# Two GNN layers on one core: the operands of the degree count change places

## The chip, the cores and the metric

The kernel runs on one NeuronCore of a Trainium2 chip. The metric is the device time of one execution in microseconds; three runs of the kernel before gave 4552.12 us in the median (4550.2 to 4552.79). The profile is another execution, taken with the hardware profiler on.

## The reference

The network has two layers on 6250 nodes with 256 features and 106,250 edges (each of 50,000 drawn pairs in both directions, and a loop for each node, sorted by destination). A layer is a graph part plus a linear-attention part, each on the layer-normalised features, and then a feed-forward part with experts. The change touches the graph convolution of the first layer alone:

```
out_deg = segment_sum(ones, src)          # edges that leave each node
in_deg  = segment_sum(ones, dst)
norm_src, norm_dst = rsqrt(max(out_deg, 1)), rsqrt(max(in_deg, 1))
x   = features * norm_src @ W_gcn         # 6250 x 64
agg = segment_sum(x[src], dst)
h   = relu(agg * norm_dst + b_gcn) @ W_out + b_out
```

To gather rows of `x`, the kernel must first have `out_deg`: for each node, how often it occurs in the list `src`.

## The kernel before, in words

Nodes lie in 49 tiles of 128 (W = 49, P = 128): node number = 128 * high part + low part. The edge list has 832 columns of 128 edges (GB = 832), padded with a node number that no tile holds. The kernel is a row of stages with a barrier of all engines between two of them. The first is the class `Front`; behind it come `Prelude` (keys and values of the attention, first groups of edges), `fold0`, `Stage1`, a table stage, `Stage2`, the router's table and `Stage3`. Each engine has its own list of instructions, written out by hand, and semaphores order them against each other.

Front does four things beside each other: it normalises the 49 node tiles, transposes them and multiplies them by W_gcn; it counts `src` into degrees; it sorts out which 128-edge blocks belong to which node tile; and it writes the table from which edges gather.

The degree count (lines 697 to 703 and 823 to 832) goes in 52 rounds, called halves in the code, of 16 columns of edges (BAT = 16). In each, VectorE (DVE) writes two one-hot tiles in bf16: `ohlo` [128, 128, 16] compares each edge's low part with 0..127 (L827), `ohhi` [128, 49, 16] its high part with 0..48 (L830). The 16 columns are the innermost axis of both, so that one column's one-hot is read at a step of 16 elements. Both tiles are doubled: round h may be written when round h - 2 has been used (`s_used`). TensorE (PE) then takes `degree(h)`: 16 products, one per column, that add up in one PSUM bank `deg`. In a product the first operand is loaded into the array as weights, the second streams through it. `deg` is opened by a product of zeros (L719) that sets all its entries.

PE's list in Front is: the zero product, then for h = 0 to 51 `degree(h)`, and from h = 3 (TILE_AT) on, behind it, `tile(h - 3)`: two f32 transposes of the next node tile (L223, into `pt`) and the two f32 products by W_gcn (L714, four matmul instructions in the trace). At three rounds there are small products for the sorting into the bank `pz` (L729 to L738). ScalarE (ACT) copies transposes and products out of PSUM (L211, L763), normalises the next tile (L772) and, in the first half of the stage, counts edges per tile by the sign function (L757, 49 times). SyncE (SP) stores each transposed tile to memory.

DVE's list, from h = 2 on: at given rounds other work (layer-norm statistics of the next seven tiles, the bias rows, the sorting), then the two one-hots of round h. When the last round is used it takes the maximum of `deg` with 1 (L1000), ScalarE the root (L798), DVE the reciprocal into `nsrc` (L1005, [128, 49]: low part on the partitions, high part along the row). Between maximum and reciprocal DVE does `put(0)` and `put(1)` (L939, L940): casts of the slot lists that PE transposes at the end of its list (L744, L745). After the reciprocal the 49 x 64 products are scaled by `nsrc` and stored as the table in seven blocks.

Of the kernel before, what the change touches and what calls it, by code (L numbers as in the profile page):

```python
# [10 lines left out]
ALU = mybir.AluOpType  # L11
ACT = mybir.ActivationFunctionType
# [3 lines left out]
P = 128  # L16
# [3 lines left out]
W = -(-N // P)  # L20
# [125 lines left out]
class Norm:  # L146
# [71 lines left out]
    def tensor(self, t, i, j):  # L218
        t.wait_ge(self.s_xn, TPI * i + j + 1)

        t.wait_ge(self.s_xr, TPI * i + (j - 1 if j >= 2 else 0))
        for c in range(C):
            mm = t.transpose(self.pt[:, j % 2, c * P:(c + 1) * P], self.xn[:, j, c * P:(c + 1) * P], self.R.ident[:, :])  # L223
        mm.then_inc(self.s_tp, 1)
# [321 lines left out]
class Front:  # L546
# [10 lines left out]
    def __init__(self, f, nc, R, A):  # L557
# [24 lines left out]
        self.ohhi = f.sb("ohhi", [P, 2, W, self.BAT], BF16)  # L582
        self.zero = f.sb("zero", [P, P], BF16)
        self.std = f.sb("dstd", [P, W])
        self.wext = f.sb("wext", [P, C, GCN])
        self.gsum = f.sb("gsum", [P, C, 2 * HEADS])
        self.bsum = f.sb("bsum", [PARTS, 2 * HEADS])
# [107 lines left out]
    def tensor(self, t):  # L695
        R, nm = self.R, self.nm

        def degree(h):
            t.wait_ge(self.s_hot, 2 * h + 2)
            for b in range(self.BAT):  # L700
                mm = t.matmul(self.deg[:, 0:W], self.ohlo[:, h % 2, :, b], self.ohhi[:, h % 2, :, b], start=False,
                              stop=False, skip_group_check=True)
            mm.then_inc(self.s_used, 1)

        def tile(n):
            i, j = divmod(n, TPI)
            if n + 1 < W:
                t.wait_ge(nm.s_xt, n + 1 if j + 1 == TPI else n)
                nm.tensor(t, *divmod(n + 1, TPI))
            t.wait_ge(nm.s_xt, n + 1)  # L710
            if n >= 2:
                t.wait_ge(self.s_ec, n - 1)
            for c in range(C):
                mm = t.matmul(self.pext[:, n % 2, 0:GCN], nm.xt[:, nm.place(i, j), c], self.wext[:, c, :], start=(c == 0),  # L714
                              stop=(c == C - 1))
            mm.then_inc(self.s_ep, 1)

        t.wait_ge(self.s_zeroed, 1)
        t.matmul(self.deg[:, 0:W], self.zero[:, :], self.zero[:, 0:W], start=True, stop=False, skip_group_check=True)  # L719
        for h in range(self.HALVES):  # L720
            degree(h)
            if h == self.TILE_AT:
                t.wait_ge(self.s_w, 16)
                nm.tensor(t, 0, 0)
            if h >= self.TILE_AT:
                tile(h - self.TILE_AT)
            if h == self.COUNT_AT:
                t.wait_ge(self.s_counted, 1)
                t.matmul(self.pz[:, 0:W], R.ones[:, :], self.cnt[:, :], start=True, stop=True).then_inc(self.s_summed, 1)  # L729
            if h == self.KEYS_AT:  # L730
                t.wait_ge(self.s_keyed, 1)
                for k in range(3):
                    t.transpose(self.pz[0:W, k * P:(k + 1) * P], self.row[:, k, :], R.ident[:, :])
                t.transpose(self.pz[0:W, 3 * P:4 * P], self.key[:, :], R.ident[:, :]).then_inc(self.s_columns, 1)
            if h == self.RANKS_AT:
                t.wait_ge(self.s_moved, 1)
                for k in range(3):
                    mm = t.matmul(self.pz[:, k * W:(k + 1) * W], self.col[0:W, k, :], self.move[0:W, :], start=True, stop=True)  # L738
                mm.then_inc(self.s_ordered, 1)
        for j in range(self.J):  # L740
            t.wait_ge(self.s_split, 2 * (j + 1))
            if j >= 2:
                t.wait_ge(self.s_put, 2 * (j - 1))
            t.transpose(self.pt[:, j % 2, 0:P], self.srcf[:, j], R.ident[:, :])  # L744
            t.transpose(self.pt[:, j % 2, P:2 * P], self.dstf[:, j], R.ident[:, :]).then_inc(self.s_turned, 1)  # L745
# [3 lines left out]
    def scalar(self, a):  # L749
        R, nm = self.R, self.nm  # L750
        self.w = 0

        def signs(n):
            for w in range(self.w, min(self.w + n, W)):
                if w:
                    a.wait_ge(self.s_signed, w)
                a.activation(self.junk[:, :], self.dstw[:, :], ACT.Sign, bias=self.edge[:, w:w + 1],  # L757
                             accum_out=self.cnt[:, w:w + 1]).then_inc(self.s_signed, 1)
            self.w = min(self.w + n, W)

        def taken(n):
            a.wait_ge(self.s_ep, n + 1)
            a.activation(self.xw[:, n, :], self.pext[:, n % 2, 0:GCN], ACT.Copy).then_inc(self.s_ec, 1)  # L763

        def normalise(i, j):
            if i >= ITER:
                return
            n = TPI * i + j
            a.wait_ge(nm.s_rstd, i + 1)
            if i:  # L770
                a.wait_ge(nm.s_tp, n - TPI + 1)
            a.activation(nm.xn[:, j], R.X[:, n, :], ACT.Identity, bias=R.less[:, n:n + 1],  # L772
                         scale=nm.rstd[:, j:j + 1]).then_inc(nm.s_xn, 1)

        a.wait_ge(self.s_cut, 1)
        signs(8)
        nm.scalar_root(a, 0)
        for j in range(TPI):
            normalise(0, j)
        for n in range(W):  # L780
            i, j = divmod(n, TPI)
            if i >= self.SETS:
                a.wait_ge(self.s_ep, TPI * (i - self.SETS) + j + 1)
                a.wait_ge(self.s_xd[nm.place(i, j)], 16 * (i // self.SETS))
            nm.scalar_copy(a, i, j)
            if n:
                taken(n - 1)
            signs(2)
            if j == 1 and i + 1 < ITER:
                nm.scalar_root(a, i + 1)  # L790
            if j >= 2:
                normalise(i + 1, j - 2)
            if j == TPI - 1:
                normalise(i + 1, j - 1)
                normalise(i + 1, j)
        taken(W - 1)
        a.wait_ge(self.s_maxed, 1)
        a.activation(self.std[:, :], self.std[:, :], ACT.Sqrt).then_inc(self.s_rooted, 1)  # L798

        def cast(i, k):  # L800
            if 0 <= i < ITER:
                x = self.xw[:, TPI * i:TPI * (i + 1), :]
                if k == 0:
                    a.wait_ge(self.s_scaled, i + 1)
                    if i >= self.TABS:
                        a.wait_ge(self.s_out[i % self.TABS], 16 * (i // self.TABS))
                else:
                    a.wait_ge(self.s_less, i + 1)
                a.activation(self.tabt[:, i % self.TABS, :, k * GCOL:k * GCOL + GCN], x, ACT.Copy)\
                    .then_inc(self.s_cast[k], 1)  # L810

        for i in range(ITER + 1):
            cast(i, 0)
            cast(i - 1, 1)
# [3 lines left out]
    def vector(self, v):  # L818
        R, nm, J, last = self.R, self.nm, self.J, W - 1
        st = Steps(v, self.s_st)  # L820
# [114 lines left out]
        def put(j):  # L935
            if j >= J:
                return
            v.wait_ge(self.s_turned, j + 1)
            v.tensor_copy(R.gsrc[:, j * P:(j + 1) * P], self.pt[:, j % 2, 0:P]).then_inc(self.s_put, 1)  # L939
            v.tensor_copy(R.gdst[:, j * P:(j + 1) * P], self.pt[:, j % 2, P:2 * P]).then_inc(self.s_put, 1)  # L940
# [56 lines left out]
                split()  # L997
            one_hots(h)
        v.wait_ge(self.s_used, self.HALVES)
        st.then(v.tensor_scalar(self.std[:, :], self.deg[:, 0:W], 1.0, None, ALU.max))  # L1000
        v.sem_inc(self.s_maxed, 1)
        put(0)
        put(1)
        v.wait_ge(self.s_rooted, 1)
# [2640 lines left out]
```

## Time and profile before

| | |
|---|---|
| median of 3 runs | 4552.12 us |
| span of the profiled execution (its only time) | 5387.9 us |
| PE busy | 3828.0 us, 71% |
| DVE busy | 3145.7 us, 58% |
| POOL busy | 2781.9 us, 52% |
| ACT busy | 2409.6 us, 45% |

The profiled execution is longer than the runs; durations and distances in its trace are those of this execution. A busy share is an average over all stages, so for a change in one stage the trace of that stage is what counts. PE in the rows is the product itself, PEld the loading of its first operand; the two overlap. `128*128 128x49` behind a product gives the loaded operand's rows and columns and then the moving operand's. In a timeline, neighbouring instructions of one line and engine are merged: start, time from the first start to the last end, and count. The printed clock (PEclk) is a share of full speed.

### The profile page before, as it was taken

The page shows a single profiled execution, that of the slowest core. Times are in us where ns is not written, and L with a number is a line of the kernel's source. Part 1 is how long each engine was busy: PE and PEld are TensorE (multiplying, and loading weights), DVE is VectorE, ACT ScalarE, POOL GpSimd, SP SyncE. Part 2 cuts the span into 40 slices and gives each one's busy share as a digit, 9 for nine tenths or more (in the row PEclk, how much of TensorE's full clock was granted, in tenths as well). Part 3 has the DMA queues.
Part 4 walks back from the last instruction along what each step waited for, and adds up shares of the span by engine and source line. Part 5 has one row for each costly group of instructions (what it writes and reads, how often), then busy time and mean ns, then how long its engine had stood idle before and what let it go on. Part 6 is the DMA issues. An engine that isn't in the chain of part 4 may idle for free. (4 is left out here: it accounts for less than half of the span.)

```text
span 5387.9 us, 67250 instructions
## 1 busy us (share of the span) xinstructions
PE 3828.0 (71%) x17777; PEld 2450.6 (45%) x17779; DVE 3145.7 (58%) x10032; ACT 2409.6 (45%) x5559; POOL 2781.9 (52%) x2880
## 2 busy tenths in 40 slices
PE   7587789889888995676777678522666666666663
PEld 7444455556555653344444445421433333333342
DVE  7564556454454655776767767734555555555556
ACT  6232222223222333787877633323444544444444
POOL 0362656565554103666666666446555555555552
PEclk9997999999999997989888888655788788787877
DMA  2322111111111005444444455231111111111111
GB/s 91 75 71 82 40 31 41 28 39 38 29 37 24 10 31 142 115 122 117 119 118 120 125 136 136 78 83 28 30 30 31 29 31 30 30 28 29 30 30 23
DMA packets 291737, 331.29 MB, mean 61 GB/s; under 512 B 80182, under 2 KB 246062, under 8 KB 291366
## 3 DMA queue, kind: packets, MB, share of 16 engines
q0 software_dynamic: 105328, 175.77, 15.2%
q1 hardware_dynamic: 186038, 151.23, 10.1%
q8 instruction: 153, 2.51, 0.2%
q14 instruction: 218, 1.79, 0.1%
HBM read 289.56 MB, written 30.77 MB: 59 GB/s over the span
## 5 line engine op out<-in xcount | busy, mean ns | idle before, releaser
L3108 POOL DMA_INDIRECT st_rows<-tabr,router_rsrc x1072 | 1022.6, 954 | 750.6 <-DVE st_part L3306 447.8
L2438 POOL DMA_INDIRECT all_XT<-tab,graph_gsrc x880 | 843.7, 959 | 482.6 <-issue 236.7
L1455 POOL DMA_INDIRECT st_rows<-tab,graph_gsrc x748 | 735.1, 983 | 570.1 <-PE st_pe L1478 299.1
L2468 PE MATMUL st_po<-all_XT,st_hot 128*128 128x264 f32 x1760 | 569.8, 471 | 152.8 <-issue 85.7
L1704 ACT ACTIVATE st_h<-st_ph,st_shift,st_scale 128x448 f32<-128x448 f32 x448 | 320.7, 724 | 733.7 <-PE st_ph L1566 519.9
L3165 PE MATMUL st_py<-st_w,st_hid 128*128 128x256 f32 x1568 | 527.2, 489 | 55.0 <-issue 50.9
L3127 PE MATMUL st_pad<-st_adr,st_hott 128*128 x1072 | 68.8, 177 | 678.7 <-DVE st_zd L3279 536.6
L2678 DVE TENSOR_TENSOR gat_sum<-gat_sum,st_po 128x264 f32 x880 | 376.2, 428 | 200.4 <-remote 79.6
L2468 PEld LDWEIGHTS st_po<-all_XT,st_hot 128*128 128x128 f32 x1760 | 343.7, 222 | 293.1 <-issue 200.0
L3165 PEld LDWEIGHTS st_py<-st_w,st_hid 128*128 128x128 f32 x1568 | 367.4, 247 | 124.2 <-issue 59.1
L3153 PE MATMUL st_px<-all_XT,st_w 128*128 128x512 f32 (+2 forms) x832 | 406.1, 635 | 18.3 <-ACT st_hid L3213 12.9
L3202 ACT ACTIVATE st_rows<-st_d 128x16 f32<-128x16 f32 x268 | 57.9, 216 | 785.2 <-DVE st_d L3289 603.2
L3127 PEld LDWEIGHTS st_pad<-st_adr,st_hott 128*128 128x128 bf16 x1072 | 51.2, 100 | 778.6 <-issue 771.1
L1579 PE MATMUL st_po<-all_XT,st_h 128*128 128x256 f32 x1568 | 374.9, 387 | 14.5 <-DVE all_X L1895 5.1
L1566 PE MATMUL st_ph<-st_h,all_XT 128*128 128x448 f32 x896 | 372.8, 566 | 13.5 <-ACT st_h L1704 11.8
L1566 PE MATMUL st_ph<-st_xt,all_XT 128*128 128x448 f32 x896 | 367.0, 560 | 18.5 <-ACT st_h L1704 17.4
L3314 DVE TENSOR_TENSOR router_racc<-router_racc,st_po 128x60 f32 x1072 | 230.4, 215 | 225.2 <-DMA all_XT<-in_m_wout 144.7
L1791 DVE TENSOR_TENSOR gcn_acc<-gcn_acc,st_pe 128x65 f32 x748 | 166.2, 222 | 332.5 <-PE st_pe L1478 223.7
L1579 PEld LDWEIGHTS st_po<-all_XT,st_h 128*128 128x128 f32 x1568 | 292.2, 192 | 68.1 <-issue 23.8
L2655 DVE TENSOR_TENSOR all_XT<-all_XT,st_wps 128x1024 f32<-128x1024 f32 x220 | 267.3, 1215 | 22.3 <-remote 21.5
L1895 DVE SCALAR_TENSOR_TENSOR all_X<-st_po,st_gate,all_X 128x256 f32 x392 | 169.5, 478 | 143.5 <-PE st_po L1579 89.7
L1566 PEld LDWEIGHTS st_ph<-st_h,all_XT 128*128 128x128 f32 x896 | 175.6, 201 | 168.9 <-issue 140.8
(517 smaller groups left out, 7453.3 us busy)
## 6 DMA issues: line engine op xcount, KB each, us to landing
st_bc<-drowr SPq DMA_DIRECT2D x268, 128.0 KB
st_bc<-drow SPq DMA_DIRECT2D x220, 128.0 KB
st_rows<-tabr,router_rsrc POOLq DMA_INDIRECT x1072
all_XT<-tab,graph_gsrc POOLq DMA_INDIRECT x880
st_xtb<-xtd SPq DMA_DIRECT2D x98, 128.0 KB
st_rows<-tab,graph_gsrc POOLq DMA_INDIRECT x748
tab<-gat_sum SPq DMA_DIRECT2D x7, 924.0 KB
xtd<-all_XT SPq DMA_DIRECT2D x49, 128.0 KB, 1.7
```

Of the source, the lines that this page charges most:

```text
L1455: g.indirect_dma_start(self.rows[:, b, u, :], None, self.R.tab0, bass.IndirectOffsetOnAxis(self.R.gsrc[:, t:t + 1], 0)).then_inc(self.s_ro ...
L1566: mm = t.matmul(self.ph[:, m % 3, 0:HALF], (self.w1, self.w2)[l][:, e, i, fb * P:(fb + 1) * P], src[:, i, h * HALF:(h + 1) * HALF], start= ...
L1579: mm = t.matmul(self.po[:, q % 2, j - 2 * k, :], self.h2[:, i, j * P:(j + 1) * P], self.wo[:, e, i, :], start=(i == 0), stop=(i == C - 1))
L1704: a.activation((self.h1, self.h2)[l][:, fb, h * HALF:(h + 1) * HALF], self.ph[:, m % 3, 0:HALF], ACT.Relu, bias=self.shift[:, l, i:i + 1], ...
L2438: g.indirect_dma_start(self.rows[:, b, u, :], None, self.R.tab1, bass.IndirectOffsetOnAxis(self.R.gsrc[:, t:t + 1], 0)).then_inc(self.s_ro ...
L2468: t.matmul(self.po[:, m % self.BANKS, 0:GROW], self.hot[:, q % self.HOTF, u], self.rows[:, q % self.ROWS, u, :], start=True, stop=True).th ...
L2655: v.tensor_tensor(m, m, self.wps[:, :, :].unsqueeze(3).to_broadcast([P, GROUP, GH, GC]), ALU.mult)\
L2678: v.tensor_tensor(aw, aw, self.po[:, (GROUP * q + u) % self.BANKS, 0:GROW], ALU.add).then_inc(self.s_acc, 1)
L3108: g.indirect_dma_start(self.rows[:, b, u, :], None, self.R.tabr, bass.IndirectOffsetOnAxis(self.R.rsrc[:, t:t + 1], 0)).then_inc(self.s_ro ...
L3153: mm = t.matmul(self.px[:, i, 0:n * P], self.w1[:, e, c, fb * P:(fb + 1) * P], R.XT[:, c, r * P:(r + n) * P], start=(c == 0), stop=(c == C ...
L3165: t.matmul(self.py[:, m % 2, 0:D], self.hid[:, (E1 * u + e) % 2, fb, j * P:(j + 1) * P], self.w2[:, e, fb, :], start=(fb == 0), stop=False)
L3314: v.tensor_tensor(aw, aw, self.po[:, q % self.SUMB, u * n:(u + 1) * n], ALU.add).then_inc(self.s_acc, 1)
```

## The change

The loaded and the moving operand of the degree products change places. `deg` then holds the count with the high part on 49 partitions and the low part along the row, [49, 128]. The maximum is taken in that form into a new tile `degt`, and a new transpose on PE brings it back to [128, 49] in the bank `pz`, from which ScalarE takes the root. The transpose stands in PE's list behind the last tile and before the slot transposes, and waits for the maximum (`s_maxed`); a new semaphore `s_degs` tells ScalarE that it is done.

```diff
+        self.degt = f.sb("degt", [P, P])
+        self.s_degs = f.sem("degs")
...
-                mm = t.matmul(self.deg[:, 0:W], self.ohlo[:, h % 2, :, b], self.ohhi[:, h % 2, :, b], start=False,
+                mm = t.matmul(self.deg[0:W, 0:P], self.ohhi[:, h % 2, :, b], self.ohlo[:, h % 2, :, b], start=False,
                               stop=False, skip_group_check=True)
...
-        t.matmul(self.deg[:, 0:W], self.zero[:, :], self.zero[:, 0:W], start=True, stop=False, skip_group_check=True)
+        t.matmul(self.deg[0:W, 0:P], self.zero[:, 0:W], self.zero[:, :], start=True, stop=False, skip_group_check=True)
...
+        t.wait_ge(self.s_maxed, 1)
+        t.transpose(self.pz[:, 0:W], self.degt[0:W, :], R.ident[0:W, 0:W]).then_inc(self.s_degs, 1)
         for j in range(self.J):
...
-        a.wait_ge(self.s_maxed, 1)
-        a.activation(self.std[:, :], self.std[:, :], ACT.Sqrt).then_inc(self.s_rooted, 1)
+        a.wait_ge(self.s_degs, 1)
+        a.activation(self.std[:, :], self.pz[:, 0:W], ACT.Sqrt).then_inc(self.s_rooted, 1)
...
-        st.then(v.tensor_scalar(self.std[:, :], self.deg[:, 0:W], 1.0, None, ALU.max))
-        v.sem_inc(self.s_maxed, 1)
+        v.tensor_scalar(self.degt[0:W, :], self.deg[0:W, 0:P], 1.0, None, ALU.max).then_inc(self.s_maxed, 1)
```

## Rows read from the trace of the kernel before

**Rows 1.** First line of the page, the whole execution.

```profile
span 5387.9 us, 67250 instructions
```

**Rows 2.** Windows of Front: start:end, length; busy of PE, PEld, DVE, ACT, POOL; PEclk; DMA.

```profile
36.80:84.00 47.20, 41.88 (x327) 40.34 (x328) 40.55 (x85) 42.74 (x103) 0.00 (x0) 1.00 0.12 41
84.00:187.00 103.00, 96.90 (x764) 95.53 (x762) 77.79 (x174) 45.83 (x126) 9.46 (x7) 1.00 0.17 54
```

**Rows 3.** Waits in Front, 36.8 to 187 us: total us, times, longest us.

```profile
ACT all_XT L211 <- PE front_pt L223: 52.9, 29, 5.1
...
PE front_deg L701 <- DVE front_ohhi L830: 13.9, 8, 3.1
DVE front_ohlo L827 <- PE front_deg L701: 13.0, 19, 1.5
```

**Rows 4.** DVE's one-hots by line, 36.8 to 186.8 us: busy us, mean ns, idle before.

```profile
L827 DVE TENSOR_TENSOR front_ohlo<-front_count,front_lo 128x2048 bf16<-128x2048 bf16 x48 | 58.7, 1222 | 14.6 <-PE front_deg L701 13.0 <-issue 1.0 <-DVE front_key L888 0.2
...
L830 DVE TENSOR_TENSOR front_ohhi<-front_count,front_hi 128x784 bf16<-128x784 bf16 x48 | 26.9, 560 | 0.0
```

**Rows 5.** Timeline of one steady period: start us, us, engine, line, out<-in.

```profile
112.18 1.72 PEld L701 LDWEIGHTS front_deg<-front_ohhi,front_ohlo 128*128 128x128 bf16 x16
...
112.39 1.73 PE L701 MATMUL front_deg<-front_ohhi,front_ohlo 128*128 128x49 bf16 x16
...
114.89 0.38 PEld L701 LDWEIGHTS front_deg<-front_ohhi,front_ohlo 128*128 128x128 bf16 x2
```

**Rows 6.** Degree and zero products, whole trace: ns min/median/max, first and last start, form.

```profile
L701 PEld LDWEIGHTS front_deg<-front_ohhi,front_ohlo x832: 142/148/295, 21.4 to 186.4; 128*128 128x128 bf16 x167
L701 PE MATMUL front_deg<-front_ohhi,front_ohlo x832: 269/278/306, 21.4 to 186.5; 128*128 128x49 bf16 x167
...
L719 PEld LDWEIGHTS front_deg<-front_zero x1: 104/104/104, 11.5 to 11.5; 128*128 128x128 bf16 x1
L719 PE MATMUL front_deg<-front_zero x1: 223/223/223, 11.5 to 11.5; 128*128 128x49 bf16 x1
```

**Rows 7.** Contiguous moving bf16 operands, later stages: ns min/median/max.

```profile
L1478 PEld LDWEIGHTS st_pe<-st_rows,st_hot x2244: 110/114/152, 535.7 to 1794.3; 128*128 128x128 bf16 x187
L1478 PE MATMUL st_pe<-st_rows,st_hot x2244: 190/196/262, 536.1 to 1794.3; 128*128 128x65 bf16 x187
...
L1544 PE MATMUL st_side<-ahead_bop,st_gt x49: 269/273/421, 582.5 to 1937.4; 96*128 96x256 bf16 x49
```

**Rows 8.** The same f32 transpose at the end of Front and later: ns min/median/max.

```profile
L745 PE MATMUL front_qpt<-all_ident,all_XT x7: 421/421/421, 187.6 to 194.3; 128*128 128x128 f32 x7
...
L2126 PE MATMUL tab_qpt<-all_ident,all_XT x9: 272/273/273, 2075.9 to 2089.5; 128*128 128x128 f32 x9
```

**Rows 9.** Timeline of PE, the first four bursts.

```profile
21.42 3.37 PE L701 MATMUL front_deg<-front_ohhi,front_ohlo 128*128 128x49 bf16 x32 [9.67 <-DVE front_ohhi L830]
31.98 1.75 PE L701 MATMUL front_deg<-front_ohhi,front_ohlo 128*128 128x49 bf16 x16 [7.20 <-DVE front_ohhi L830]
36.82 1.75 PE L701 MATMUL front_deg<-front_ohhi,front_ohlo 128*128 128x49 bf16 x16 [3.08 <-DVE front_ohhi L830]
```

**Rows 10.** Timeline of the end of Front, behind the last burst.

```profile
186.54 1.05 PE L714 MATMUL front_pext<-front_wext,all_XT 128*128 128x64 f32 x4
186.76 0.21 DVE L1000 TENSOR_SCALAR front_dstd<-front_deg 128x49 f32<-128x49 f32 x1 [2.94 <-PE front_deg L701]
...
187.39 0.42 PE L744 MATMUL front_qpt<-all_ident,all_XT 128*128 128x128 f32 x1
...
187.60 0.42 PE L745 MATMUL front_qpt<-all_ident,all_XT 128*128 128x128 f32 x1
...
187.75 0.24 ACT L798 ACTIVATE front_dstd<-front_dstd 128x49 f32<-128x49 f32 x1
...
188.27 0.28 DVE L940 CAST graph_gdst<-front_qpt 128x128 bf16<-128x128 f32 x1
...
188.89 0.46 DVE L1005 RECIPROCAL graph_nsrc<-front_dstd 128x49 f32<-128x49 f32 x1
```

## The prediction

> **What bounds the kernel now.** I read the busy time by stretch first, then the waits of the first stage, its costliest lines and last its timeline. The profiled execution has one time, its span of 5387.9 us [rows 1]; the runs' median is 4552.1 us, 0.845 of it. Nothing in the page says where the profile stretched the rest, so I work out a difference in the profile's microseconds and add it to the median.
>
> The change lies in Front, the first 207 us or so. From 36.8 us on, PE alternates a burst of 16 degree products with one tile (two transposes, then the products for the table). It is busy 41.88 of 47.2 us and then 96.90 of 103.0 us [rows 2]. DVE waits for degree bursts 19 times, 13.0 us, ScalarE for PE's transposes 52.9 us, and PE for a one-hot 13.9 us [rows 3]. So Front is bound by PE's queue with some gaps. In the steady part the period is 2.71 us, from one burst's first weight load to the next one's, 112.18 to 114.89 us [rows 5]. DVE's one-hots are 1.22 + 0.56 = 1.78 us of a period [rows 4].
>
> Inside the period, the 16 matmuls of a burst span 1.73 us and the last of them takes about 0.27, so fifteen spacings fill 1.46 us: 97 ns from product to product [rows 5, 6]. From the fourth burst at 36.82 us [rows 9] to the last maximum at 186.76 us [rows 10] there are 149.9 us; 49 x 2.71 = 132.8 us are periods, 13.9 us the waits, the remaining 3 us the small products for sorting.
>
> **Which operand sets the 97 ns?** Both are read at a step of 16 elements (32 bytes), the loaded one 128 columns wide, the moving one 49. The loads first: 148 ns here, 104 ns for the zero matrix read in one piece [rows 6], 114 ns in stage 1 at a step of 4 elements [rows 7]. The stride costs a load 44 ns. Then the products: the zero one, the same 128x49 read in one piece, took 223 ns, the degree ones 269 at least and 278 in the median [rows 6], so 46 to 55 ns more for 49 columns, 0.94 to 1.12 ns each. Loads and products overlap: 16 loads of 148 ns in a row would be 2.37 us, and a burst takes 1.73 [rows 5, 6]. So the slower of the two sets the spacing, and I read that as the moving read.
>
> What a column costs without stride depends on the clock. The stretches of Front print 1.00 [rows 2], but transposes of 128x128 f32 take 421 ns in Front and 272 ns at 2076 us [rows 8]. I take Front to run at the 1.2 GHz level in spite of the print. Contiguous bf16 products of 65 and 256 columns last 190 and 269 ns at the other level [rows 7]: 79/191 = 0.41 ns a column, 0.83 at half the clock. A strided moving column then costs 0.83 + 0.94 to 1.12 = 1.77 to 1.95 ns; 49 of them take 87 to 96 of the 97 ns and leave 1 to 10 ns fixed.
>
> **The change part by part.**
>
> *The degree products, 832 of them.* The moving operand grows from 49 to 128 columns. The trace has no strided moving read of 128 columns. From below: one column a cycle without penalty, 128 x 0.83 = 106 ns. From above: 128 x 1.95 = 250 ns with today's whole load of 148 ns [rows 6] exposed ahead of it, 398 ns. Between: 128 x 1.77 + 10 = 237, 128 x 1.95 + 1 = 251, and by plain proportion 97 x 128/49 = 253. The nearest rows are the degree products themselves; I take 240 ns, near the end that the undisturbed minimum of 269 gives. Each product costs PE's queue 143 ns more, a burst 2.29 us, and the period becomes 5.0 us.
>
> Two rules of the Trainium skill pull apart here. Its page "TensorE: Matmul & The Clock Gate" (Back-to-back issue gap) sets the spacing by columns alone, N/1.2 ns when cold: an estimated 107 ns at 128 columns. By that rule 49 columns would need 41 ns where the rows show 97, so this trace speaks against it. The page "SBUF — State Buffer" (Specifications) gives lines of 16 bytes and a penalty for each step to a new one; the 46 to 55 ns agree, and by it the wider operand should not be the one that streams. By the first rule the sum is that of the third rival, by the second that of the forecast.
>
> *The first three bursts* are covered. The first two start at 21.42 us and end at 24.8; the third starts at 31.98, since DVE does statistics and tables in between [rows 9]. Two bursts of 3.9 us end at 29.2 us, the third at 35.9, before the fourth's start at 36.82. Cost nothing; without that cover 3 x 2.29 = 6.9 us.
>
> *The other 49 bursts* are on the path: 49 x 2.29 = 112.2 us more. Against it stand the 13.9 us in which PE waited for one-hots. The longest such wait was 3.1 us [rows 3]; DVE may be two bursts ahead, and two periods grow by 4.6 us, so all of it should go under. ScalarE's 42.74 us of the first stretch [rows 2] fit easily as the stretch grows. 112.2 - 13.9 = 98.3 us.
>
> *The tail.* The maximum reads 49 x 128 from PSUM in place of 128 x 49: 0.28 us by the 128x128 cast, 0.07 more than its 0.21 [rows 10]; it lies beside the last table products, 186.54 to 187.59 us. The new transpose waits for that maximum in PE's queue; behind it stand the 14 slot transposes, and DVE's casts and reciprocal wait for those. PE comes to it after the table products, when the maximum is done, and it takes about one spacing of the slot transposes, 187.39 to 187.60 us: 0.21 us [rows 10]. ScalarE's root, at 187.75 us now, needs its end, so starts some 0.2 us later; the reciprocal at 188.89 us stands behind casts that move by the same 0.21 [rows 10]. Bounds: 0, if the table blocks behind it wait for their stores anyway, and 0.7 us for transpose and root in series (0.42 + 0.24). I take 0.3. No DMA is added, and none is moved past another on SP's or POOL's queue; SP's stores of transposed tiles only spread over a longer stage.
>
> *Sum:* 98.3 + 0.3 = 98.6 us, 5486.5 us in the profile. On the median: 4651 us, 2.2% slower. Had the profile stretched Front as much as the whole, it would be 98.6 x 0.845 = 83 us, 4635 us.
>
> **The rivals.**
>
> 1. *Both strided reads share one path*, so the extra costs add: 44 for the load and 46 to 55 for the product come near the 97 ns, which speaks for it. Then the load sheds 79/128 of 44, 27 ns, and the product gains 79 x 1.02, 81 ns: 151 ns. 784 x 54 ns = 42.3, less 13.6: 29 us, 4581 us. Against: the undisturbed product of 269 ns has the whole surplus without a load beside it.
> 2. *The load is exposed*, half of it or all: 324 to 398 ns, 784 x 227 = 178 us or 784 x 301 = 236 us, less 13.6: 4716 to 4774 us. For it: no bf16 load of fewer than 128 columns is in these rows, so its overlap is unseen. Against: the overlap above. On the width the same TensorE page says (Weight-path perf modes) that the fast load is for 128 columns that are not f32; no run here shows what 49 do.
> 3. *One column a cycle*, 107 ns: 784 x 10 = 7.8 us, which the 13.9 us of waits can swallow: 4552 to 4557 us, no change. From 97 + 13.9/0.784 = 115 ns on, every nanosecond reaches the end. Against: 223 and 269 ns for one shape.
> 4. *The other side: Front's clock rises to 2.4 GHz*, because the burst's gaps close. Place: Front from the fourth burst on. Strided columns at half price give 120 ns and the tile half of its 1.05 us, a period of 2.5 us; next is DVE's work, 40.55 + 77.79 us for 49 periods [rows 2], 2.4 us each. 49 x 0.2 = 10 us gone: 4542 us. It decides only if the clock rises and products then come at under 115 ns or nearly so. For it: the rows show that the operation can run at 272 ns. Against: PE's gaps were already few from 84 us on, and its transposes at Front's end still took 421 ns [rows 8].
>
> That the change doesn't do what it says can't be: shapes and operands are fixed in the code.
>
> **How the numbers follow.** The forecast has 0.76, the shared path 0.07, the exposed load 0.07, one column a cycle 0.05, the faster clock 0.05. Within the forecast 205 to 275 ns a product give 71 to 126 us, 4623 to 4678 us. I set 4618 to 4690 us: below for a Front that is shorter in the runs than in the profile, above for a load that is exposed in part. A measurement of this kernel can tell 0.2% from no change, 9 us. Slower by more: 0.90 (forecast, shared path, exposed load); within: 0.05 (one column a cycle); faster: 0.05 (the clock).
>
> **What would show it.** Degree products 240 ns apart and about 410 ns long, a burst of some 3.9 us, a period of 5 us, the last maximum near 285 us; PE without waits for one-hots from the fourth burst on; DVE's waits for degree bursts, 13.0 us now [rows 3], grown to some 100 us; f32 transposes in Front still at 421 ns; the stages behind it shifted and otherwise as they were. It is wrong if products come at under 115 ns, if those transposes fall to 272 ns, or if Front's later end does not arrive at the kernel's end.

## The result and the profile after

The changed kernel takes 4656.19 us (median of 5 runs, 4651.93 to 4659.53) against 4551.3 us beside it (5 runs, 4543.5 to 4552.79): a ratio of 1.0234, 95% interval 1.0221 to 1.0246, or 105 us. The forecast was 4651 us, the range 4618 to 4690 us. The profiled execution of the changed kernel spans 4654.5 us, so this profile isn't stretched. For the kernel before I took a second profile (span 4550.9 us, first experiment below); its Front agrees with the first one's to 0.3 us up to the last maximum.

First the waits of the changed kernel in Front (engine, line, who it waited for: us in total, times, longest), the answer to [rows 3]. Its lines stand two to four higher: L703 is the degree product (L701 before), L716 the table product (L714).

```profile
ACT all_XT L211 <- PE front_pt L223: 151.9, 48, 7.5
DVE front_ohlo L831 <- PE front_deg L703: 107.4, 39, 3.6
PEld front_pt L223 <- issue: 19.3, 48, 0.4
```

DVE waits 107.4 us for degree bursts, 13.0 before; ScalarE 151.9 us for PE's transposes, 52.9 before. No wait of PE for a one-hot is left among the first lines. The third row is new: 48 times, 0.4 us each, the loading of weights stands idle ahead of a transposes' load, with no releaser in sight. PE's busy time by stretch, of the changed kernel, with the columns of [rows 2]:

```profile
36.80:84.00 47.20, 46.75 (x195) 34.07 (x195) 25.40 (x53) 27.10 (x62) 0.00 (x0) 1.00 0.08 26
84.00:187.00 103.00, 103.00 (x433) 76.33 (x433) 47.15 (x97) 46.16 (x109) 0.00 (x0) 1.00 0.08 26
187.00:295.00 108.00, 108.00 (x455) 80.10 (x453) 47.73 (x109) 19.20 (x56) 8.20 (x7) 1.00 0.11 34
```

```profile
106.34 3.48 PEld L703 LDWEIGHTS front_deg<-front_ohlo,front_ohhi 128*49 128x49 bf16 x16
106.34 3.96 PE L703 MATMUL front_deg<-front_ohlo,front_ohhi 128*49 128x128 bf16 x16
...
110.23 0.29 PEld L223 LDWEIGHTS front_pt<-all_ident,all_XT 128*128 128x128 f32 x2 [0.40 <-issue]
110.23 0.69 PE L223 MATMUL front_pt<-all_ident,all_XT 128*128 128x128 f32 x2
...
110.50 0.98 PEld L716 LDWEIGHTS front_pext<-front_wext,all_XT 128*128 128x128 f32 x4
110.71 0.95 PE L716 MATMUL front_pext<-front_wext,all_XT 128*128 128x64 f32 x4
...
111.60 3.96 PE L703 MATMUL front_deg<-front_ohlo,front_ohhi 128*49 128x128 bf16 x16
```

The period is 111.60 - 106.34 = 5.26 us (2.71 before). The burst spans 3.96 us; with a last product of 0.41 us fifteen spacings fill 3.55, 236 ns each. That last product starts at 109.89 us, and the transposes' load at 110.23: the standstill of the third row of the waits. The durations of the changed kernel's products in ns, min/median/max, against [rows 6]:

```profile
L703 PEld LDWEIGHTS front_deg<-front_ohlo,front_ohhi x832: 167/169/192, 21.8 to 296.2; 128*49 128x49 bf16 x167
L703 PE MATMUL front_deg<-front_ohlo,front_ohhi x832: 411/413/460, 21.8 to 296.4; 128*49 128x128 bf16 x167
L721 PEld LDWEIGHTS front_deg<-front_zero x1: 118/118/118, 11.8 to 11.8; 128*49 128x49 bf16 x1
L721 PE MATMUL front_deg<-front_zero x1: 302/302/302, 11.8 to 11.8; 128*49 128x128 bf16 x1
```

A product takes 413 ns, the zero product of the same shape, read in one piece, 302. PE's timeline of the changed kernel over the first four bursts, against [rows 9]:

```profile
21.80 7.69 PE L703 MATMUL front_deg<-front_ohlo,front_ohhi 128*49 128x128 bf16 x32 [9.71 <-DVE front_ohhi L834]
32.37 3.96 PE L703 MATMUL front_deg<-front_ohlo,front_ohhi 128*49 128x128 bf16 x16 [2.88 <-DVE front_ohhi L834]
37.21 3.96 PE L703 MATMUL front_deg<-front_ohlo,front_ohhi 128*49 128x128 bf16 x16 [0.88 <-DVE front_ohhi L834]
```

The timeline of all its engines behind the last burst, against [rows 10]:

```profile
296.90 0.28 DVE L1004 TENSOR_SCALAR front_degt<-front_deg 49x128 f32<-49x128 f32 x1 [8.80 <-PE front_deg L703]
...
297.84 0.34 PE L743 MATMUL front_pz<-all_ident,front_degt 49*128 49x49 f32 x1
...
298.21 0.21 ACT L802 ACTIVATE front_dstd<-front_pz 128x49 f32<-128x49 f32 x1
...
299.67 0.46 DVE L1008 RECIPROCAL graph_nsrc<-front_dstd 128x49 f32<-128x49 f32 x1
```

The first burst starts at 21.80 us (21.42 before) and the fourth at 37.21 (36.82). The last maximum comes at 296.90 us (186.76). From there to the reciprocal it takes 2.77 us, 2.13 before; in Front's last rows that is gone: VectorE's last instruction of Front ends 19.6 us behind the maximum, at 316.5 us, and 20.3 and 21.3 us behind it in the two profiles of before, where DVE and ScalarE wait for the stores of the table. The f32 transposes at Front's end still take 421 ns; here they are in the changed kernel, against [rows 8]:

```profile
L749 PE MATMUL front_qpt<-all_ident,all_XT x7: 421/421/421, 298.4 to 305.0; 128*128 128x128 f32 x7
```

### The profile page after: what moved, and what is told of

The parts are those of the page before. It is cut to its first block and busy times, and to the rows that moved or that the text cites. A ratio compares the mean times of both kernels' runs of the same rounds, so it can differ in the third digit from the quotient of the medians.

```text
span 4654.5 us, 67253 instructions
## 1 busy us (share of the span) xinstructions
PE 3747.9 (81%) x17780; PEld 2382.2 (51%) x17780; DVE 3143.3 (68%) x10032; ACT 2411.6 (52%) x5559; POOL 2787.3 (60%) x2880
## 5 line engine op out<-in xcount | busy, mean ns | idle before, releaser
L2471 PE MATMUL st_po<-all_XT,st_hot 128*128 128x264 f32 x1760 | 522.8, 445 | 107.6 <-DVE gat_sum L2681 103.1
L3168 PE MATMUL st_py<-st_w,st_hid 128*128 128x256 f32 x1568 | 444.5, 433 | 2.3 <-ACT st_hid L3216 2.3
L2471 PEld LDWEIGHTS st_po<-all_XT,st_hot 128*128 128x128 f32 x1760 | 306.2, 205 | 247.0 <-issue 112.8
L3156 PE MATMUL st_px<-all_XT,st_w 128*128 128x512 f32 (+2 forms) x832 | 394.9, 622 | 16.4 <-ACT st_hid L3216 16.4
L3168 PEld LDWEIGHTS st_py<-st_w,st_hid 128*128 128x128 f32 x1568 | 319.8, 215 | 51.7 <-ACT st_hid L3216 2.4
L3156 PEld LDWEIGHTS st_px<-all_XT,st_w 128*128 128x128 f32 x832 | 164.1, 208 | 173.0 <-issue 146.3
```

Source lines behind the costliest of these rows:

```text
L2471: t.matmul(self.po[:, m % self.BANKS, 0:GROW], self.hot[:, q % self.HOTF, u], self.rows[:, q % self.ROWS, u, :], start=True, stop=True).th ...
L3156: mm = t.matmul(self.px[:, i, 0:n * P], self.w1[:, e, c, fb * P:(fb + 1) * P], R.XT[:, c, r * P:(r + n) * P], start=(c == 0), stop=(c == C ...
L3168: t.matmul(self.py[:, m % 2, 0:D], self.hid[:, (E1 * u + e) % 2, fb, j * P:(j + 1) * P], self.w2[:, e, fb, :], start=(fb == 0), stop=False)
```

## The experiments

All kernels ran beside the kernel before; where a ratio stands, its 95% interval is behind it. In b_move1, b_load1, a_move1, a_load1, a_move4 and a_move8 the products read other one-hot values than they should, with the shapes and the work of their base; the others compute everything. The spacings are worked out as above, from a burst's span. Where a cut shows a product, it shows its changed operands alone.

**Second profile of the kernel before** (b_again). Edit: none.

> The kernel before, unchanged, for a second profile: the first one's span was 5387.9 us, so its later stages can't be laid beside those of the changed kernel. Expected by all theories: a span near 4550 us, and in Front the same picture: degree products 97 ns apart, a period of 2.71 us, the last maximum at 187 us, Front's end at 207 us. If Front's end differs by more than 2 us, part of the 109.4 us between the two Fronts is the profile's.

The end of Front in the timeline of this second profile, with the two instructions that bound its tail:

```profile
186.97 0.21 DVE L1000 TENSOR_SCALAR front_dstd<-front_deg 128x49 f32<-128x49 f32 x1 [2.97 <-PE front_deg L701]
...
189.09 0.45 DVE L1005 RECIPROCAL graph_nsrc<-front_dstd 128x49 f32<-128x49 f32 x1
```

4552.65 us. The last maximum at 186.97 us, the period 2.71 to 2.73 us, the end of Front at 208.3 us. The first profile had stretched later stages, not Front.

**The moving operand of before in one piece** (b_move1).

```diff
-  self.ohhi[:, h % 2, :, b]
+  self.ohhi[:, h % 2].rearrange("p w b -> p (w b)")[:, b * W:(b + 1) * W]
```

> The kernel before with one edit: the moving operand (49 columns) is read in one piece instead of at a step of 16 elements. It reads other one-hot values than it should, so the degrees are wrong; work and shapes stay. Theory, the strided moving read sets the 97 ns: the product falls from 278 to about 225 ns (the zero product's 223), the spacing to what the load allows, 55 to 75 ns, the period by 16 x 0.03 = 0.5 us, and Front becomes bound by VectorE: 10 to 25 us less, 4527 to 4541 us. Rival, the load of 128 strided columns sets it: the spacing stays 97 ns, 4551 us. Rival, both share one path: 97 - 50 = 47 ns, a gain at the upper end.

The products' durations in b_move1 (ns, min/median/max), and behind them a burst in PE's timeline:

```profile
L701 PEld LDWEIGHTS front_deg<-front_ohhi,front_ohlo x832: 141/166/292, 21.9 to 175.3; 128*128 128x128 bf16 x167
L701 PE MATMUL front_deg<-front_ohhi,front_ohlo x832: 220/238/272, 21.9 to 175.3; 128*128 128x49 bf16 x167
```

```profile
110.83 1.17 PE L701 MATMUL front_deg<-front_ohhi,front_ohlo 128*128 128x49 bf16 x16
```

4537.03 us against 4548.71, 0.9974 (0.9963 to 0.9985). Products last 220 ns at least (269 before) and stand 62 ns apart; a load takes 166 ns now. The last maximum comes at 175.6 us, 11.4 earlier. The moving read had set the 97. That the load sets the 62 is shown further down, where b_both4 changes its step as well.

**The loaded operand of before in one piece** (b_load1): the same edit on `ohlo`.

> The kernel before with one edit: the loaded operand (128 columns) is read in one piece instead of at a step of 16 elements (degrees wrong, work and shapes the same). Theory, the moving read sets the spacing and the load hides: loads fall from 148 to about 104 ns, the spacing stays at 97 ns, 4551 us, no change. Rival, the load sets it: spacing 50 to 70 ns, 10 to 25 us less. Rival, shared path: 97 - 44 = 53 ns, likewise 10 to 25 us less.

The same two views of b_load1:

```profile
L701 PEld LDWEIGHTS front_deg<-front_ohhi,front_ohlo x832: 102/127/276, 22.0 to 184.2; 128*128 128x128 bf16 x167
L701 PE MATMUL front_deg<-front_ohhi,front_ohlo x832: 248/271/277, 22.0 to 184.3; 128*128 128x49 bf16 x167
```

```profile
111.75 1.64 PE L701 MATMUL front_deg<-front_ohhi,front_ohlo 128*128 128x49 bf16 x16
```

4548.09 us, 0.9996 (0.9987 to 1.0006): no difference. Loads fall to 127 ns, the spacing from 97 to 91. So 6 ns of the 97 go with the step of the loaded operand, too little to be seen at the kernel's end, and 91 ns belong to the 49 moving columns: 1.86 ns each. The shared path, which asked for 53 ns, falls.

**The moving operand of the changed kernel in one piece** (a_move1): the same edit on its `ohlo`.

> The changed kernel with one edit: the moving operand (128 columns) is read in one piece instead of at a step of 16 elements (degrees wrong, work and shapes the same). Theory, the step makes the whole difference: products of about 300 ns (the zero product took 302), 107 to 110 ns apart at the 1.2 GHz level, a period of 16 x 0.108 + 1.47 = 3.2 us; against 2.71 us 24 us more, of which waits swallow 14: 4560 us or so. If the clock rises with it, products 56 ns apart, transposes at 272 ns, VectorE next: about 4540 us. Rival, the width alone costs it, not the step: spacing stays 236 ns, 4656 us.

A burst early in PE's timeline of a_move1, and a period from later on:

```profile
44.11 1.96 PE L703 MATMUL front_deg<-front_ohlo,front_ohhi 128*49 128x128 bf16 x16
...
112.66 0.44 PE L223 MATMUL front_pt<-all_ident,all_XT 128*128 128x128 f32 x2
...
113.42 1.71 PE L703 MATMUL front_deg<-front_ohlo,front_ohhi 128*49 128x128 bf16 x16
115.06 0.44 PE L223 MATMUL front_pt<-all_ident,all_XT 128*128 128x128 f32 x2
```

Busy times by stretch in a_move1, with the columns of [rows 2], the first one of the time of that early burst:

```profile
37.00:45.00 8.00, 7.95 (x54) 7.01 (x54) 3.52 (x8) 5.56 (x15) 0.00 (x0) 0.50 0.11 35
36.80:84.00 47.20, 40.80 (x327) 37.00 (x327) 40.49 (x85) 42.23 (x102) 0.00 (x0) 0.79 0.12 40
84.00:187.00 103.00, 91.38 (x776) 84.00 (x775) 81.34 (x186) 46.21 (x131) 9.61 (x7) 0.91 0.17 55
```

4544.08 us against 4548.71, 0.9991 (0.9982 to 1.0001). Without the step the whole 105 us is gone, but not by the step alone: the clock rose with it. The two transposes take 0.44 us together (0.69 in the changed kernel) and four of the seven of L749 at Front's end 272 ns: Front now runs at the 2.4 GHz level for the most part, and its stretches print 0.79 and 0.91, from records that begin at 25.5 us. The early burst lies in a stretch of 0.50; its last product takes 0.31 us, and the spacing is (1.96 - 0.31)/15 = 110 ns, as expected for one column a cycle at that level. In the later one it is (1.71 - 0.26)/15 = 97 ns, and 94 from product to product in the median of all. If the stream still set it there, it would be half of the 110, an estimated 55 ns. So something else does, and what is left is the load of 49 columns at a step of 16, 191 ns long; that is argued, for no run reads both operands in one piece. I had expected 4560 us for the low level, so an estimated 16 us of the way back are the clock's.

**The loaded operand of the changed kernel in one piece** (a_load1): the same edit on its `ohhi`.

> The changed kernel with one edit: the loaded operand (49 columns) is read in one piece instead of at a step of 16 elements (degrees wrong, work and shapes the same). Theory, the load hides behind the 236 ns of the moving read: loads shorten from 169 ns towards 118 (the zero product's), the spacing stays 236 ns, 4656 us. Rival, the load is exposed in part: the spacing falls by what the load sheds, 50 ns, 0.8 us a period, 39 us less, 4617 us. Rival, shared path: 17 ns, 13 us less.

The products' durations in a_load1:

```profile
L703 PEld LDWEIGHTS front_deg<-front_ohlo,front_ohhi x832: 117/142/146, 21.3 to 292.6; 128*49 128x49 bf16 x167
L703 PE MATMUL front_deg<-front_ohlo,front_ohhi x832: 408/412/413, 21.3 to 292.8; 128*49 128x128 bf16 x167
```

4652.92 us, 1.0224 (1.0207 to 1.0241). The load falls from 169 to 142 ns and the spacing from 236 to 232, 1.81 ns a column. Of the 27 ns that the load sheds 4 reach the spacing, so it is nearly hidden in the changed kernel; a gain of 3 us, if any, cannot be told from none at the kernel's end.

**The loaded operand padded to 128 columns** (a_load128).

```diff
-        self.ohhi = f.sb("ohhi", [P, 2, W, self.BAT], BF16)
+        self.ohhi = f.sb("ohhi", [P, 2, P, self.BAT], BF16)
...
-  t.matmul(self.deg[0:W, 0:P], ...)
+  t.matmul(self.deg[:, 0:P], ...)      # columns 49 to 127 of ohhi set to 0 once
```

The one-hot is still written to 49 columns, and the zero product is widened to 128 too.

> The changed kernel with one edit: the one-hot of the high part is padded with zero columns to 128, so that 128 columns are loaded again, not 49; the counts stay as they are, on 49 of 128 partitions. In the changed kernel the transposes behind a burst start their load 340 ns after the last degree product's start, and the first degree load behind the tile 349 ns after the last tile product's; in the kernel before both follow within 2 ns. Theory, a change of the loaded width between products drains PE: the padded kernel has no such wait, its period falls from 5.25 to about 4.9 us, 16 us less, 4640 us, with the spacing at 236 ns still. Rival, the wait comes from the long strided stream itself: it stays, 4656 us. If the load of 49 had been exposed within a burst, the spacing moves as well.

A period of the timeline in a_load128:

```profile
112.35 4.02 PE L703 MATMUL front_deg<-front_ohlo,front_ohhi 128*128 128x128 bf16 x16
...
115.96 0.43 PEld L223 LDWEIGHTS front_pt<-all_ident,all_XT 128*128 128x128 f32 x2
116.19 0.61 PE L223 MATMUL front_pt<-all_ident,all_XT 128*128 128x128 f32 x2
...
117.33 0.90 PE L703 MATMUL front_deg<-front_ohlo,front_ohhi 128*128 128x128 bf16 x3
```

4644.6 us, 1.0213 (1.0196 to 1.023), 11.6 us under the 4656.19 of the changed kernel; the last maximum is at 283.9 us, 13.0 earlier. The transposes' load starts at 115.96 us, inside the burst, without a standstill, and the period is 4.98 us at a spacing of 240. The products stand 4.2 ns further apart (240.5 against 236.3 in the mean), 3.3 us in all, so the standstills that went were worth some 16 us. The standstill in the changed kernel goes with the change between 49 and 128 loaded columns. Whether it is the width itself or the way in which loads of 128 are done, the run doesn't tell.

**Steps of 4 and 8 elements for the changed kernel's moving operand** (a_move4, a_move8; one run each).

```diff
-  self.ohlo[:, h % 2, :, b]
+  self.ohlo[:, h % 2].rearrange("p e b -> p (e b)").rearrange(
+      "p (k e s) -> p k e s", e=P, s=4)[:, b // 4, :, b % 4]       # s=8: b // 8, b % 8
```

> The changed kernel with one edit: the moving operand is read at a step of 4 elements (8 bytes) instead of 16 (degrees wrong, work and shapes the same). If a column costs extra when it is the only one in its 16 bytes, two columns share them here: spacing near that of the read in one piece, 107 to 130 ns, about 4560 to 4575 us. If any step costs the same: 236 ns, 4656 us.

> The changed kernel with one edit: the moving operand is read at a step of 8 elements (16 bytes) instead of 16 (degrees wrong, work and shapes the same). If the cost is one per 16 bytes touched: every column has its own 16 bytes, as at a step of 16, spacing 236 ns, 4656 us. If it grows with the distance, or counts 32 bytes: less, between 107 and 200 ns.

PE's timeline in a_move4, a burst early in Front, and a later one with the transposes behind it:

```profile
72.41 2.11 PE L703 MATMUL front_deg<-front_ohlo,front_ohhi 128*49 128x128 bf16 x16
...
112.97 2.11 PE L703 MATMUL front_deg<-front_ohlo,front_ohhi 128*49 128x128 bf16 x16
115.01 0.44 PE L223 MATMUL front_pt<-all_ident,all_XT 128*128 128x128 f32 x2
```

The stretch around the early burst in a_move4, with the columns of [rows 2]:

```profile
69.00:75.70 6.70, 6.70 (x44) 6.24 (x44) 6.31 (x12) 4.02 (x9) 0.00 (x0) 0.50 0.06 20
```

PE's timeline in a_move8, a burst and the transposes behind it:

```profile
111.32 3.90 PE L703 MATMUL front_deg<-front_ohlo,front_ohhi 128*49 128x128 bf16 x16
115.15 0.69 PE L223 MATMUL front_pt<-all_ident,all_XT 128*128 128x128 f32 x2
```

At a step of 4: 4553.54 us, under the 4560 to 4575 expected, spacing (2.11 - 0.30)/15 = 121 ns, and the high clock again for the most part (transposes 0.44 us). At a step of 8: 4647.55 us, (3.90 - 0.41)/15 = 233 ns, as at a step of 16 (236). So distance doesn't count; what counts is how many pieces of 16 bytes a read touches: 128 at steps of 8 and 16, 64 at a step of 4. 233/128 = 1.82 and 121/64 = 1.89 ns a piece. The clock doesn't change the price: in a_move4 the early burst, in a stretch of 0.50, spans 2.11 us like the later one.

**The layout for a step of 4** (b_both4, b_hi4, a_both4). From the price per piece followed a version that should beat both kernels.

```diff
-        self.ohlo = f.sb("ohlo", [P, 2, P, self.BAT], BF16)
-        self.ohhi = f.sb("ohhi", [P, 2, W, self.BAT], BF16)
+        self.ohlo = f.sb("ohlo", [P, 2, 4, P, 4], BF16)
+        self.ohhi = f.sb("ohhi", [P, 2, 4, W, 4], BF16)
...
-            v.tensor_tensor(self.ohlo[:, h % 2], self.count[:, :, :],
-                            self.lo[:, col:col + self.BAT].unsqueeze(1).to_broadcast([P, P, self.BAT]),
+            v.tensor_tensor(self.ohlo[:, h % 2], self.count[:, :, 0:4].unsqueeze(1).to_broadcast([P, 4, P, 4]),
+                            self.lo[:, col:col + self.BAT].rearrange("p (k s) -> p k s", s=4).unsqueeze(2).to_broadcast([P, 4, P, 4]),
                             ALU.is_equal).then_inc(self.s_hot, 1)        # ohhi likewise with W
...
-  self.ohlo[:, h % 2, :, b], self.ohhi[:, h % 2, :, b]
+  self.ohlo[:, h % 2, b // 4, :, b % 4], self.ohhi[:, h % 2, b // 4, :, b % 4]
```

> The kernel before with both one-hots laid out so that a column's one-hot is read at a step of 4 elements (8 bytes): tiles [128, 4, 128, 4] and [128, 4, 49, 4]; the full computation. Theory, one price per 16 bytes touched, about 1.85 ns: the moving read touches 25 pieces in place of 49, 46 ns, the load is no longer behind it, spacing 45 to 60 ns; VectorE writes the same number of elements in runs of four, 1.22 and 0.56 us as now, and is next: Front some 12 us shorter, 4538 us, a little below the 4537 us of the kernel whose moving operand alone was read in one piece, or equal to it. If VectorE loses its pace by the new layout (2.1 and 0.8 us), it takes the place of PE: 4551 us or more. If the clock of Front rises as it did with denser streams, the tile shrinks as well, but VectorE still sets the end.

> The kernel before with the layout for step 4 in the high part's one-hot alone (the moving operand, 49 columns); the loaded operand is still read at a step of 16; the full computation. Spacing by the strided load, 62 ns as with the moving operand in one piece, 4537 us. If the load at a step of 16 hides behind nothing else, it is 2 to 5 us behind the kernel with both laid out anew; if VectorE already sets the end, the same.

> The changed kernel (49 columns loaded, 128 moving) with the same layout for both one-hots, read at a step of 4 elements; the full computation. By the price per 16 bytes the moving read touches 64 pieces: 118 to 121 ns apart, as with the moving operand alone at this step; the drain at the change of the loaded width stays (0.3 us a period at the low clock). 4545 to 4560 us: the exchange of operands costs 100 us only through the step of 16, and is still 5 to 15 us behind the kernel before in the same layout. Rival, loading fewer columns pays once the step is small: as fast as that one, 4538 us.

The timeline of DVE and PE in b_both4 around one burst:

```profile
113.28 0.56 DVE L830 TENSOR_TENSOR front_ohhi<-front_count,front_hi 128x784 bf16<-128x784 bf16 x1
113.76 1.22 DVE L827 TENSOR_TENSOR front_ohlo<-front_count,front_lo 128x2048 bf16<-128x2048 bf16 x1
...
113.90 0.96 PE L701 MATMUL front_deg<-front_ohhi,front_ohlo 128*128 128x49 bf16 x16 [3.25 <-DVE front_ohhi L830]
```

The wait of PE for one-hots in b_both4's Front (total us, times, longest), against [rows 3]:

```profile
PE front_deg L701 <- DVE front_ohhi L830: 30.4, 14, 3.9
```

Before in the new layout: 4529.17 us against 4544.13, 0.9964 (0.9951 to 0.9978), better than both kernels. VectorE keeps its 1.22 and 0.56 us, a burst spans 0.96 us, (0.96 - 0.23)/15 = 49 ns a product, and now PE waits for one-hots 30.4 us (13.9 before): VectorE sets the pace of Front more than it did. The maximum comes at 167.4 us, 19.6 earlier, more than the 12 I expected. With the high part's one-hot alone: 4534.68 us, 0.998 (0.997 to 0.9989), maximum at 175.5 us, as b_move1: the strided load's 62 to 64 ns are the next bound there, not yet VectorE, since a loaded operand at a step of 4 brings 49 ns and a maximum 8.1 us earlier.

The changed kernel in the new layout: 4547.43 us, 1.0008 (0.9999 to 1.0018), 116 ns a product, the maximum at 190.2 us. The exchange of the operands then costs 18 us by the medians (5 to 15 expected), against 105 us at a step of 16; the clock is in that too, for from 84 to 187 us Front prints 0.90 here and 0.67 in b_both4.

## Why the prediction was right

*The step that carried it held.* I had read the 97 ns as the price of the moving columns from two durations, 269 and 223 ns of one shape. b_move1 and b_load1 show it apart: without the moving step 62 ns, without the loaded step 91. The price of a strided column came to 1.77 to 1.95 ns; measured 1.86 (91/49) and 1.81 (232/128). It isn't made up as I had it, though, of 0.83 ns that go with the clock and 0.94 to 1.12 ns of stride: in a_move4 the price of a piece is the same at both levels, so the 120 ns of the fourth rival would not have come with a faster clock either. I took 240 ns a product, it is 236, and (236.3 - 97.9) x 784 = 108.5 us with the means of all bursts (112.2 forecast).

*What was wrong in the sum.* The sentence "the period becomes 5.0 us" left out what the change of the loaded width does at each border between burst and tile: there the next load starts late, and PE stands still. The trace has 5.25 us, at a spacing of 236.3 ns: 0.33 us for 49 periods, 16 us, that I had priced at nothing; a_load128 takes it back, 13.0 us at the last maximum and 3.3 us that its wider spacing costs. In [rows 5] the loads run on into the next product group without a break, and I never asked whether they would for a load of another shape; the second rival had this doubt for loads inside a burst, where it is unfounded (a_load1).

*The cover.* That DVE's lateness would go under held: PE waits 0.88 us before the fourth burst and then never. The 13.9 us taken off for it were counted wrongly: 3.1 of them end at the fourth burst [rows 9], so they lie outside the 149.9 us, and 10.9 are left in it; the "remaining 3 us" of the prediction are 6. What went under shows better in the waits of the loads, in the kernel before from 37.2 to 187 us:

```profile
PEld front_deg L701 <- DVE front_ohhi L830: 12.5, 9, 3.3
```

With 1.5 us of waits for ScalarE's copies beside it, of which the changed kernel keeps 0.4, that is 13.6 us; that 13.9 comes near it is luck. 108.5 + 16.1 - 13.6 = 111.0 us, and the maximum moved by 110.1 (296.90 - 186.76; "near 285" in the forecast), by 109.8 against the fourth burst. The first three bursts cost nothing: the fourth starts 0.39 us later, and so does the first one, 0.38.

*The tail.* 0.64 us to the reciprocal, where I had 0.3 and an upper bound of 0.7; it vanishes before Front ends, the lower bound.

*From Front to the end.* The forecast was 98.6 us; the maximum moved by 110.1, Front's end by 108.2 (316.5 - 208.3 in the second profile), the runs by 105. The last two agree within the interval of the ratio (100.6 to 112 us), and the runs of the kernel before differ by 9 us among themselves; the 3 us between them stay open. So that 4651 lies near 4656 is in part luck: the standstills of 16 us, left out of the sum, were made up for in part, by products that grew by 138.4 ns instead of 143 (3.6 us in all) and by some 5 us that did not arrive at the end. The forecast scaled by the first profile's stretch, 4635 us, was wrong: Front wasn't stretched.

*The clock.* Front is at the 1.2 GHz level in both kernels by its transposes, under a print of 1.00 that stands for no record. The fourth rival's effect exists, but not by its cause: the transposes of L749 fall to 272 ns in the median, the 2.4 GHz level, in a_move1 and to 273 in a_move4 and a_both4, and b_both4 is at that level in parts of its Front (transposes of L223 from 272 to 474 ns). All four read the moving operand at a step of 1 or 4, but so do b_move1 and b_hi4, whose transposes stay at the low level through Front (417 ns at least at L223, 421 at L745). In the changed kernel, where PE is busy for 257.75 of 258.2 us, and in a_move8 they stay at 421. What the chip goes by, these runs don't settle.

*One column a cycle.* The rule of the Trainium skill on the back-to-back gap ("TensorE: Matmul & The Clock Gate", Back-to-back issue gap), which the section gives for single products and not for a stream with loads, gave an estimated 107 ns and the trace 236. It comes out in a_move1's bursts at the low level (110 ns), and doesn't hold for operands read at a step of 8 or 16 elements, nor at a step of 4 with the clock at its high level (121 ns). The Trainium skill's rule of lines ("SBUF — State Buffer", Specifications) does hold, to the size of 16 bytes: the steps of 8 and 16 cost the same, the step of 4 half. Two hits per line, which it asks for full bandwidth, are not enough at the high level: the step of 4 has two and takes 121 ns, the read in one piece 97 or less.

## What to carry to other kernels

Before two operands of a product change places, count for each how many pieces of 16 bytes a read of it touches: here 1.8 to 1.9 ns each for the moving one, whatever the clock. The wider operand may stream only if its columns lie close; laying out one-hots in runs of four cost VectorE nothing here and gained 15 us. And in one PE queue the loaded width should change seldom, since a pair of borders between 49 and 128 columns cost 0.33 us at the 1.2 GHz level.
